# A new prologue and operand layout, and where SyncE issues the loads of second operand halves

## The chip, the core and the metric

The kernel runs on one core of a Trainium2 chip. The metric is device time in microseconds (us); less is better. The core has TensorE (matrix products), VectorE, ScalarE and GpSimd, and SyncE, which issues the DMA transfers; 16 DMA engines carry them.

## What is computed

One transformer layer on x of shape (2, 1024, 128): layer norm, attention of 16 heads of size 8 with a relative position bias and a causal mask, residual; then layer norm, a feed-forward of width 512 (only expert 0 counts), its own residual and layer norm, residual.

```python
q, k, v = (xn @ W.T + b) per head             # 2 batches, 16 heads, 1024 x 8
sim = q @ k.T + rel_emb[bucket(i - j)] * 8 ** -0.5   # no other scale
attn = softmax(where(j > i, -inf, sim)); x = x + (attn @ v) @ Wo.T + bo
t = layernorm(x); h = relu(t @ w1[0] + b1[0]); y = t + h @ w2[0] + b2[0]
out = x + layernorm(y) * gamma + beta
```

## The kernel before

**Operands.** q and k are split into three bfloat16 parts each. All nine products of parts come out of one matmul whose contraction runs over 3 x 3 x 8 = 72 rows of the tiles QA and KA, padded with zeros to 96 rows (KS). Rows 96 and 97 (MROW) of QA hold minus the row maxima, against rows of ones in KA, so that the second pass of scores comes out with the maximum already subtracted. The parts go through a DRAM scratch (qk_scratch): `store_q` and `store_k` write them (L361 to L372), `load_half` (L374) reads one half (512 of 1024 columns) of the operands of one group back, each part at three places. It issues four DMAs: three of 24 rows for QA and one of 72 rows for KA, every row 4 KB.

**Groups.** The 32 pairs of batch and head are worked on as 8 groups of 4 heads. For each group TensorE first makes plain scores in 39 "units" (`unit`, L980): VectorE takes row maxima of them (L759 far from the diagonal, L766 near it, where the bias table NB is added). Unit 13 ("m", 0) and unit 38 ("m", 1) turn the finished maxima of the first and second 512 rows into rows, VectorE copies them to mrow (L754), and `move_m` (L390) sends them to QA. Units that need the second operand half start with unit 10. Then 12 steps of transposed scores follow (L1015), with the bias added by small matmuls from TT (L1032), the exponential on ScalarE (L626) and the product with v (L1044). The units of the next group are interleaved with the steps of this one; the last, unit 38, runs after the group's own first steps. Both `move_m` have to land before the scores of their 512 rows: the second one before step 4.

**SyncE's order.** One queue, in program order. `load` (L440), once per group g: second maxima of g; first maxima of g+1; when step 8 of g has been scored, first half of g+2; when all steps of g have been scored, second half of g+2 and its bias tiles TT from DRAM (L386). From g = 4 on, the gathers of finished heads (L403, L406) stand between these.

**Prologue.** x comes in two DMAs, then a table, the early weights and some rows, and all engines wait for the lot (s_w). Layer norm (L690 to L701), transposes (L932), q/k/v (L938, L944), splits (L712 to L715). The bias table is made as 16 rows of 384, stored to DRAM and loaded back reversed into rev (L414, L422); a flip matmul (L959) and a copy (L598) per two heads give NBH. GpSimd meanwhile sets the pad rows (L482, L485). Group 0's units 0 to 24 (OWN0 = 25) come before its first scores, with the q, k, v of batch 1 (QK_AT) and six of the eight flips (FLIP_AT) between them; `move_m(0, 0, 0)` (L430) is issued behind both loads of group 1 and their TT.

## Time and profile before

| | us |
|---|---|
| median of 3 runs | 405.28 (403.5 to 411.39) |
| the profiled execution | 402.29 |
| its span, first to last instruction | 400.5 |
| mean granted TensorE clock | 0.924 |

The profile is of one execution. Busy time and idle time are given per engine; idle time matters only where that engine is the one the rest waits for. The chain of waits follows the work that ended last back from the end.

### The profile page before, as it was taken

How to read it: one execution, taken by the hardware profiler on the slowest of the kernel's cores; microseconds unless marked ns; L12 is line 12 of the kernel's file. 1: busy time of each engine (PE TensorE's matmuls, PEld its weight loads, DVE VectorE, ACT ScalarE, POOL GpSimd, SP SyncE). 2: the span in 40 equal slices, each digit the busy share in tenths (PEclk: the TensorE clock that was granted, in tenths of full speed). 3: DMA queues.
4: the chain of work that ended last, by engine and by line, in shares of the span. 5: the costliest groups of instructions: out<-in, count | busy, mean ns of one | idle time of the engine just before them, and what ended most of it. 6: DMA issues, size and time to landing. Idle time of an engine off the chain costs nothing.

```text
span 400.5 us, 8158 instructions
## 1 busy us (share of the span) xinstructions
PE 321.0 (80%) x3197; PEld 153.1 (38%) x3197; DVE 287.5 (72%) x960; ACT 184.0 (46%) x258; POOL 69.5 (17%) x78
## 2 busy tenths in 40 slices
PE   0182438396999899799889979988988998999982
PEld 0131215143334335334434433443443344337752
DVE  3985356358668589588678848967875996773986
ACT  1042024131655554575565545556555545873330
POOL 9812035700001000100100100010010000161552
PEclk9996586668699999999999989999998999999998
DMA  8013422410012101201201220331222010100011
GB/s 227 26 53 116 145 90 95 148 64 3 2 43 66 39 18 52 81 1 61 75 12 44 68 64 2 86 88 26 65 79 55 15 16 12 33 2 10 5 52 53
DMA packets 18295, 21.97 MB, mean 55 GB/s; under 512 B 5584, under 2 KB 14960, under 8 KB 18256
## 3 DMA queue, kind: packets, MB, share of 16 engines
q1 hardware_dynamic: 18256, 21.45, 18.5%
q8 instruction: 25, 0.41, 0.4%
q14 instruction: 14, 0.11, 0.1%
HBM read 14.98 MB, written 4.23 MB: 48 GB/s over the span
## 4 chain that ended last, share of the span: by engine, by line
PE 51%; DVE 17%; DMA 15%; ACT 7%; issue 5%; SPq 4%; POOL 1%; DVEq 0%; POOLq 0%; ACTq 0%
PE ps L1015 14%; PE ps L1044 13%; PE ps L1001 13%; DMA QA<-mrow 7%; ACT PT L626 6%; PE ps L1032 5%; DMA qk_scratch<-QS 4%; DVE FM L759 3%; DVE XN L701 2%; DVE junk L766 2%; DMA KA<-qk_scratch 2%; DMA rows<-in_vectors 2%; PE ps L1077 2%; DVE st L836 1%; DVE U L889 1%
## 5 line engine op out<-in xcount | busy, mean ns | idle before, releaser
L626 ACT ACTIVATE PT<-ps 128x1024 f32<-128x1024 f32 (+1 forms) x192 | 145.8, 810 | 132.4 <-PE ps L1032 101.9
L759 DVE TENSOR_REDUCE FM<-ps 128x1 f32<-128x512 f32 (+3 forms) x176 | 108.4, 660 | 29.2 <-PE ps L1001 29.1
L1001 PE MATMUL ps<-KA,QA 96*128 96x256 bf16 (+3 forms) x544 | 108.7, 294 | 17.6 <-DMA KA<-qk_scratch 14.3
L1015 PE MATMUL ps<-QA,KA 98*128 98x512 bf16 (+3 forms) x384 | 99.0, 343 | 25.4 <-DMA QA<-mrow 10.3
L766 DVE CUSTOM_DVE_ANT_0 junk<-ps,NB 128x256 bf16<-128x256 f32 (+1 forms) x224 | 78.8, 403 | 37.3 <-PE ps L1001 37.2
L1044 PE MATMUL ps<-PT,VG 128*16 128x512 f32 (+3 forms) x768 | 86.9, 498 | 0.0
L1001 PEld LDWEIGHTS ps<-KA,QA 96*128 96x128 bf16 x544 | 44.1, 101 | 103.7 <-DVE FM L759 32.9
L1015 PEld LDWEIGHTS ps<-QA,KA 98*128 98x128 bf16 x384 | 32.5, 101 | 52.5 <-ACT PT L626 21.6
L497 POOL COPY NB<-NBH 128x1024 bf16<-128x1024 bf16 x7 | 7.3, 1040 | 212.3 <-PE ps L1044 211.4
L1032 PE MATMUL ps<-TT,flb 128*32 128x176 f16 (+4 forms) x1152 | 38.9, 245 | 0.0
L1032 PEld LDWEIGHTS ps<-TT,flb 128*32 128x32 bf16 x1152 | 21.5, 96 | 17.9 <-issue 17.0
L1044 PEld LDWEIGHTS ps<-PT,VG 128*16 128x16 f32 x768 | 21.5, 97 | 10.3 <-issue 7.2
L766 DVE DVE_READ_ACCUMULATOR2_ANT FM<- 128x1 f32 x256 | 21.3, 83 | 0.0
L766 DVE CUSTOM_DVE_ANT_0 junk<-ps,NBH 128x256 bf16<-128x256 f32 (+1 forms) x32 | 11.2, 403 | 10.5 <-PE ps L1001 10.3
L932 PE MATMUL ps<-early_s,XN 128*128 128x128 f32 x16 | 4.1, 424 | 18.1 <-DVE XN L701 18.1
L1077 PE MATMUL ps<-QS,late_s 128*128 128x512 f32 x32 | 15.8, 611 | 0.8 <-ACT QS L653 0.8
L545 POOL TENSOR_SCALAR tmp<-mv 128x4 f32<-128x4 f32 x8 | 2.3, 285 | 71.3 <-DVE mv L839 71.3
L585 ACT ACTIVATE QS<-ps,early_s 128x512 bf16<-128x512 f32 x8 | 5.5, 687 | 16.4 <-PE ps L938 16.4
L701 DVE TENSOR_SCALAR XN<-X,mv,rs 128x128 f32<-128x128 f32 x16 | 11.9, 1332 | 0.1
L754 DVE COPY mrow<-ps 8x512 bf16<-8x512 bf16 x16 | 6.5, 407 | 7.2 <-PE ps L989 7.2
L938 PE MATMUL ps<-xnT,early_s 128*128 128x512 f32 x16 | 10.5, 769 | 0.0
L932 PEld LDWEIGHTS ps<-early_s,XN 128*128 128x128 f32 x16 | 3.2, 222 | 18.9 <-issue 16.4
(88 smaller groups left out, 255.5 us busy)
## 6 DMA issues: line engine op xcount, KB each, us to landing
QA<-qk_scratch SPq DMA_DIRECT2D x48, 96.0 KB
KA<-qk_scratch SPq DMA_DIRECT2D x16, 288.0 KB
TT<-f_scratch SPq DMA_DIRECT2D x16, 120.0 KB, 7.8
qk_scratch<-QS SPq DMA_DIRECT2D x4, 384.0 KB
qk_scratch<-QS SPq DMA_DIRECT2D x12, 128.0 KB
...
```

Of the source, the lines that this page charges most:

```text
L497: nc.gpsimd.tensor_copy(NB[:, p, :, :], NBH[:, bass.ds(HG * hg, HG), :]).then_inc(s_nb, 1)
L626: nc.scalar.activation(PT[:, s % 3, 2 * q:2 * q + 2, off:off + w], ST[:, q, :, off:off + w], ACT.Exp).then_inc(s_exp, 1)
L701: last = nc.vector.tensor_scalar(XN[:, t, :], X[:, t, :], mv[:, t, 0:1], rs[:, t:t + 1], ALU.subtract, ALU.mult)
L759: nc.vector.tensor_reduce(FM[:, ib, heads[0]:heads[-1] + 1, piece], bank[:, 0:w * len(heads)].rearrange("p (h n) -> p h n", n=w), AX.X, AL ...
L766: last = nc.vector.tensor_tensor_reduce(junk[:, k % NSM, i, 0:w], bank[:, i * w:(i + 1) * w], nb[:, h, 256 - w:256], 1.0, NEG, ALU.add, AL ...
L932: last = nc.tensor.transpose(ps[:, BANK["T", b, half], i * 128:(i + 1) * 128], XN[:, b * TPB + 4 * half + i, :], idf[:, :])
L938: nc.tensor.matmul(ps[:, BANK["QK"[qk], b, c], :], (wq_s, wk_s)[qk][:, :], xnT[:, b, c * IC:(c + 1) * IC], start=True, stop=True).then_inc ...
L1001: last = nc.tensor.matmul(bank[:, i * w + j - j0:i * w + j - j0 + n], QA[0:KS, p, ib // 4, h, (ib % 4) * 128:(ib % 4 + 1) * 128], KA[0:KS, ...
L1015: last = nc.tensor.matmul(ST[:, q, h % 2, off:off + w], KA[0:KST, p, jb // 4, h, (jb % 4) * 128:(jb % 4 + 1) * 128], QA[0:KST, p, ic, h, o ...
L1032: last = nc.tensor.matmul(ST[r0:r0 + 32, q, h % 2, off:off + n], flb[:, 32 * e:32 * e + 32], TT[:, p, h, u0:u0 + n], start=False, stop=Tru ...
L1044: last = nc.tensor.matmul(OV[32 * h:32 * h + 2 * HD, off:off + w], VG[:, p, jb, h, :], PT[:, s % 3, h, off:off + w], start=(jb == 0), stop ...
L1077: last = nc.tensor.matmul(bank, w1_s[:, f * 128:(f + 1) * 128], tT[:, c % 2, :], start=True, stop=True)
```

## The change

The layout drops the zero padding (72 rows, maxima in rows 72 and 73), and its 72 rows are ordered head-size first, so that a half is loaded in six DMAs of 24 rows, each with 8 as its outermost count instead of 3. q and k are stored alike, one DMA each with 128 outermost. The maxima move in one DMA instead of two. The second half of group g+1 is issued in `load(g)`, right behind the second maxima of g. TT is no longer loaded from DRAM for each group: one tile TL holds the table of all heads, and GpSimd copies 4 heads of it. In the prologue x comes in four DMAs; table and early weights are issued from ScalarE's queue; each consumer waits for what it needs; the layer norm runs in pieces of 4 tiles; the bias table is made with 128 partitions and the heads innermost (DRAM runs of 32 bytes when stored, 8 KB when loaded); all flips come before the units; GpSimd sets fewer pads and takes the third part of q. 17 units instead of 25 stand before the first scores. Not shown: buffer and semaphore declarations, the layer norm's renumbering, host code.

```diff
-KS = 96
-MROW = 96
+KS = ROWS
+MROW = ROWS
...
-QK_AT = {3: (0, 0), 5: (0, 1), 8: (1, 0), 10: (1, 1)}
-REMAINDER_AT = {6: (0, 0), 8: (0, 1), 11: (1, 0), 13: (1, 1)}
-FLIP_AT = {14: 2, 15: 3, 16: 4, 18: 5, 19: 6, 20: 7}
+QK_AT = {1: (0, 0), 3: (0, 1), 5: (1, 0), 7: (1, 1)}
+REMAINDER_AT = {4: (0, 0), 6: (0, 1), 8: (1, 0), 10: (1, 1)}
+V_AT = {9: 0, 11: 1}
 RECIP_AFTER = (6, 14, 22, 30)
-OWN0 = 25
+OWN0 = 17
...
+        TL = sb("TL", [128, NEARU, H], FP16)
...
+        R = [PT[:, 1, :, :], OT[:, 4:6, :].rearrange("p g (c n) -> p (g c) n", n=IC)]
+        rev = PT[:, 0, :, :].rearrange("p h n -> p (h n)").bitcast(BF16)
...
-            for b in range(B):
-                sp.dma_start(X[:, b * TPB:(b + 1) * TPB, :], xv[:, b * TPB:(b + 1) * TPB, :]).then_inc(s_x[b], 16)
-                if b == 0:
-                    for dst, src in [(table_s[:, :], table), (early_s[:, :], early),
-                                     (rows[:, :, :], bass.AP(vectors.tensor, 0, [[0, 128], [D, 5], [1, D]]))]:
-                        sp.dma_start(dst, src).then_inc(s_w, 16)
+            for k in range(2 * B):
+                sp.dma_start(X[:, 4 * k:4 * k + 4, :], xv[:, 4 * k:4 * k + 4, :]).then_inc(s_x[k], 16)
+                if k == 1:
+                    sp.dma_start(rows[:, :, :], bass.AP(vectors.tensor, 0, [[0, 128], [D, 5], [1, D]])).then_inc(s_rows, 16)
...
-            def store_q(b, c):
-                sp.wait_ge(s_q3[b], c * 2 + 1)
-                sp.dma_start(bass.AP(qk_d, c * CN + b * GPB * GN, [[IC, 128], [G * GN, NPART], [1, IC]]),
-                             QS[:, b, 0, :, c * IC:(c + 1) * IC]).then_inc(s_qst[b][c], 16)
-            def store_k(b, c):
-                sp.wait_ge(s_q3[b], c * 2 + 2)
-                for a in range(NPART):
-                    sp.dma_start(bass.AP(qk_d, QN + c * CN + (b * GPB * NPART + a) * GN,
-                                         [[NPART * GN, GPB], [IC, HG * HD], [1, IC]]),
-                                 QS[:, b, 1, a, c * IC:(c + 1) * IC]).then_inc(s_qst[b][c], 16)
+            PN = G * GN
+            def store(b, c, qk):
+                sp.wait_ge(s_q3[b][qk], c + 1)
+                sp.dma_start(bass.AP(qk_d, (2 * c + qk) * NPART * PN + b * GPB * GN, [[IC, 128], [PN, NPART], [1, IC]]),
+                             QS[:, b, qk, :, c * IC:(c + 1) * IC]).then_inc(s_qst[b][c], 16)
             def load_half(g, p, c):
-                rows_q = [[0, NPART], [HG * IC, HD], [1, HG * IC]]
-                rows_k = [[0, NPART], [HG * IC, NPART * HD], [1, HG * IC]]
-                for a in range(NPART):
-                    sp.dma_start(QA[24 * a:24 * a + 24, p, c, :, :].rearrange("r h n -> r (h n)"),
-                                 bass.AP(qk_d, g * GN + (c * CN + a * G * GN), rows_q)).then_inc(s_ldqk[p][c], 16)
-                sp.dma_start(KA[0:ROWS, p, c, :, :].rearrange("r h n -> r (h n)"),
-                             bass.AP(qk_d, g * (NPART * GN) + (QN + c * CN), rows_k)).then_inc(s_ldqk[p][c], 16)
-            def load_tt(hg, p):
-                for part in range(2):
-                    sp.dma_start(TT[64 * part:64 * part + 64, p, :, :],
-                                 bass.AP(f16_d, hg * (HG * 2 * BW) + part * BW, [[1, 64], [2 * BW, HG], [1, NEARU]])
-                                 ).then_inc(s_ldt[p], 16)
+                at = g * GN + 2 * c * NPART * PN
+                rows_q = [[HG * IC, HD], [PN, NPART], [1, HG * IC]]
+                rows_k = [[HG * IC, HD], [0, NPART], [1, HG * IC]]
+                for u in range(NPART):
+                    r0 = u * NPART * HD
+                    for tile, start, pattern in ((QA, at, rows_q), (KA, at + (NPART + u) * PN, rows_k)):
+                        sp.dma_start(tile[r0:r0 + NPART * HD, p, c, :, :].rearrange("r h n -> r (h n)"),
+                                     bass.AP(qk_d, start, pattern)).then_inc(s_ldqk[p][c], 16)
             def move_m(p, half, g):
                 wait_apart(sp, s_smf, NU * g + (NU - 1 if half else UNITS.index(("m", 0))) + NSM + 1)
-                for part in range(2):
-                    sp.dma_start(QA[MROW + part:MROW + part + 1, p, half, :, :],
-                                 mrow[4 * part:4 * part + 4, half, :]).then_inc(s_md[half], 16)
+                sp.dma_start(QA[MROW:MROW + 2, p, half, :, :], mrow[:, half, :]).then_inc(s_md[half], 16)
...
-            store_q(0, 0)
             sp.wait_ge(s_f, 1)
-            sp.dma_start(fr_d.ap(), Fr[:, :]).then_inc(s_fst[0], 16)
-            store_k(0, 0)
+            sp.dma_start(bass.AP(fr_d, 0, [[H, 128], [128 * H, XC], [1, H]]), Fr[:, :, :]).then_inc(s_fst[0], 16)
+            sp.wait_ge(s_f, 2)
+            for part in range(2):
+                sp.dma_start(bass.AP(f16_d, part * BW * H, [[H, 128], [128 * H, XC], [1, H]]),
+                             F16[:, part, :, :]).then_inc(s_fst[1], 16)
             sp.wait_ge(s_fst[0], 16)
-            sp.dma_start(rev[:, 0:HG, :], bass.AP(fr_d, 0, [[1, 128], [BW, HG], [1, 256]])).then_inc(s_rev[0], 16)
-            sp.wait_ge(s_f, 2)
-            sp.dma_start(f16_d.ap(), F16[:, :, :]).then_inc(s_fst[1], 16)
-            sp.wait_ge(s_zero, 5)
-            sp.wait_ge(s_qst[0][0], 64)
+            sp.dma_start(rev[:, :], bass.AP(fr_d, 0, [[H, 128], [1, 256 * H]])).then_inc(s_rev, 16)
+            store(0, 0, 0)
+            store(0, 0, 1)
+            sp.wait_ge(s_fst[1], 32)
+            sp.wait_ge(s_zero, 1)
+            sp.wait_ge(s_qst[0][0], 32)
             load_half(0, 0, 0)
-            store_q(0, 1)
-            store_k(0, 1)
-            sp.dma_start(rev[:, HG:H, :], bass.AP(fr_d, HG * BW, [[1, 128], [BW, H - HG], [1, 256]])).then_inc(s_rev[1], 16)
-            sp.wait_ge(s_qst[0][1], 64)
+            for part in range(2):
+                sp.dma_start(TL[64 * part:64 * part + 64, :, :].rearrange("r u h -> r (u h)"),
+                             bass.AP(f16_d, part * BW * H, [[H, 64], [1, NEARU * H]])).then_inc(s_tl, 16)
+            store(0, 1, 0)
+            store(0, 1, 1)
+            sp.wait_ge(s_qst[0][1], 32)
             load_half(0, 0, 1)
-            sp.wait_ge(s_fst[1], 16)
-            load_tt(0, 0)
             load_half(1, 1, 0)
...
-            def load(g, hg, p, sums=()):
+            def load(g, p, sums=()):
                 move_m(p, 1, g)
+                if g:
+                    second_half(g + 1, 1 - p)
                 for k in sums[:1]:
...
                 load_half(g + 2, p, 0)
                 for k in sums[1:]:
                     gather_all(k)
-                wait_apart(sp, s_str, 2 * NSTEP * g + 2 * NSTEP)
-                load_half(g + 2, p, 1)
-                load_tt(hg, p)
+            def second_half(g, p):
+                sp.wait_ge(s_str, 2 * NSTEP * (g - 1))
+                load_half(g, p, 1)
...
             for r in range(0, G // 2 - 2):
                 for p in range(2):
-                    load(2 * r + p, (2 * r + 2) % GPB + p, p)
-            load(G - 4, 2, 0, sums=(0, 1))
-            load(G - 3, 3, 1, sums=(2, 3))
+                    load(2 * r + p, p)
+            load(G - 4, 0, sums=(0, 1))
+            load(G - 3, 1, sums=(2, 3))
             move_m(0, 1, G - 2)
+            second_half(G - 1, 1)
             gather_all(4)
             move_m(1, 0, G - 1)
             gather_all(5)
...
         def _(pool):
-            for pad in (QA, KA):
-                nc.gpsimd.memset(pad[64:96, :, :, :, :].rearrange("p q c h n -> p (q c h n)").bitcast(F32),
-                                 0.0).then_inc(s_zero, 1)
-            pool.wait_ge(s_zero, 2)
-            nc.gpsimd.memset(KA[96:98, :, :, :, :], 1.0).then_inc(s_zero, 1)
-            pool.wait_ge(s_zero, 3)
+            nc.gpsimd.memset(KA[64:KST, :, :, :, :].rearrange("p q c h n -> p (q c h n)"), 1.0).then_inc(s_zero, 1)
+            pool.wait_ge(s_zero, 1)
             nc.gpsimd.memset(VG[:, :, :, :, :], 1.0).then_inc(s_zero, 1)
-            nc.gpsimd.memset(junk[:, :, :, :], 0.0).then_inc(s_zero, 1)
...
+            def copy_tt(hg, p):
+                nc.gpsimd.tensor_copy(TT[:, p, :, :].rearrange("p h u -> p u h"),
+                                      TL[:, :, bass.ds(HG * hg, HG)]).then_inc(s_tt, 1)
...
-            pool.wait_ge(s_w, 16 * NW)
+            for c in range(2):
+                pool.wait_ge(s_mid, 2 * c + 1)
+                q = QS[:, 0, 0, :, c * IC:(c + 1) * IC]
+                nc.gpsimd.tensor_tensor(q[:, 2, :], R[0][:, 2 * c, :], q[:, 1, :], ALU.subtract).then_inc(s_q3[0][0], 1)
...
+            pool.wait_ge(s_tl, 32)
+            copy_tt(0, 0)
+            copy_tt(1, 1)
...
+                    copy_tt((2 * r + 2) % GPB + p, p)
...
+            act.dma_start(table_s[:, :], table).then_inc(s_tab, 16)
+            act.dma_start(early_s[:, :], early).then_inc(s_early, 16)
+            act.wait_ge(s_eps, 1)
+            nc.scalar.activation(warm[:, :], eps[:, :], ACT.Sqrt).then_inc(s_warm, 1)
...
+            def copy_nbh(i):
+                act.wait_ge(s_flip, i + 1)
+                nc.scalar.copy(NBH[:, :, 32 * i:32 * i + 32],
+                               ps[:, FLIP_BANK[i], :].rearrange("p (c h) -> p h c", h=H)).then_inc(s_nbh, 1)
...
             deviation(0)
-            turned(0)
+            turned(0, 0)
             deviation(1)
-            first_parts(0)
+            act.wait_ge(s_early, 16)
+            first_parts(0, 0)
+            turned(0, 1)
+            first_parts(0, 1)
             copy_v(0)
-            copy_nbh(0, 2)
-            turned(1)
-            first_parts(1)
+            for i in range(4):
+                copy_nbh(i)
+            deviation(2)
+            deviation(3)
+            for i in range(4, 8):
+                copy_nbh(i)
+            turned(1, 0)
+            turned(1, 1)
+            first_parts(1, 0)
+            first_parts(1, 1)
             copy_v(1)
-            copy_nbh(2, 8)
             act.wait_ge(s_warm, 1)
-            nc.scalar.activation(warm[:, :], cols[:, 3:4], ACT.Exp).then_inc(s_warm, 1)
...
-            act.wait_ge(s_q3[1], 4)
...
+                mid = nc.vector.tensor_copy(q[:, 1, :], R_).then_inc(s_mid, 1)
+                if qk:
+                    dve.wait_ge(s_mid, k + 1)
+                    nc.vector.tensor_tensor(q[:, 2, :], R_, q[:, 1, :], ALU.subtract).then_inc(s_q3[0][1], 1)
+            def bias_table():
+                got = ps[:, BANK["F", 0, 0], 0:2 * XC * H].rearrange("p (a c h) -> p a c h", a=2, c=XC)
+                mask = [mk_s[:, a, :, :].broadcast_to([128, XC, H]) for a in range(2)]
+                dve.wait_ge(s_tp, TASK["F", 0, 0] + 1)
+                nc.vector.scalar_tensor_tensor(Fr[:, :, :], got[:, 1, :, :], SCALE, mask[1],
+                                               ALU.mult, ALU.add).then_inc(s_f, 1)
+                own(nc.vector.scalar_tensor_tensor(Ff[:, :, :], got[:, 0, :, :], SCALE / BSC, mask[0],
+                                                   ALU.mult, ALU.add))
+                own(nc.vector.tensor_copy(F16[:, 0, :, :], Ff[:, :, :]))
+                own(nc.vector.tensor_tensor(Ff[:, :, :], Ff[:, :, :], F16[:, 0, :, :], ALU.subtract))
+                nc.vector.tensor_scalar(F16[:, 1, :, :], Ff[:, :, :], LSC, None, ALU.mult).then_inc(s_f, 1)
...
+            dve.wait_ge(s_early, 16)
+            bias_table()
             stats0(1)
-            dve.wait_ge(s_w, 16 * NW)
+            norm(1)
...
-            split(0, 0, 0)
...
-            dve.wait_ge(s_zero, 5)
+            for c in range(2):
+                for qk in range(2):
+                    split(c, qk)
+            for k in range(2, 4):
+                stats0(k)
+            for k in range(2, 4):
+                norm(k)
...
+            def task_f():
+                for k in range(2 * XC):
+                    last = nc.tensor.matmul(ps[:, BANK["F", 0, 0], k * H:(k + 1) * H],
+                                            oh_s[:, k // XC, (k % XC) * 128:(k % XC + 1) * 128], emb_s[:, :],
+                                            start=True, stop=True)
+                last.then_inc(s_tp, 1)
...
-                pe.wait_ge(s_rev[i >= 2], 16)
                 if i >= 2:
                     pe.wait_ge(s_nbh, i - 1)
-                if FLIP_BANK[i] == 2:
-                    pe.wait_ge(s_r, 4)
-                nc.tensor.matmul(ps[:, FLIP_BANK[i], :], flb[:, 64:192], rev[:, 2 * i:2 * i + 2, :],
+                nc.tensor.matmul(ps[:, FLIP_BANK[i], :], flb[:, 64:192], rev[:, 512 * i:512 * i + 512],
...
-            pe.wait_ge(s_w, 16 * NW)
+            pe.wait_ge(s_tab, 16)
+            task_f()
+            pe.wait_ge(s_early, 16)
             task_t(0, 0)
+            task_qks(0, 0)
             task_t(0, 1)
-            task_qks(0, 0)
-            task_f(0)
-            task_f(1)
             task_qks(0, 1)
             task_v(0, 0)
             task_v(0, 1)
             pe.wait_ge(s_f, 2)
             pe.wait_ge(s_ov, 2)
             pe.wait_ge(s_cst, 2)
-            task_flip(0)
-            task_flip(1)
-            pe.wait_ge(s_q3[0], 2)
+            pe.wait_ge(s_rev, 16)
+            for i in range(8):
+                task_flip(i)
+            pe.wait_ge(s_q3[0][1], 1)
...
-                    pe.wait_ge(s_md[ic], 32 * g + 32)
...
-                            pe.wait_ge(s_ldt[1 - p], 32 * load)
+                            pe.wait_ge(s_tt, g + 2)
...
-            pe.wait_ge(s_q3[0], 4)
-            pe.wait_ge(s_nbh, 2)
+            pe.wait_ge(s_q3[0][1], 2)
+            pe.wait_ge(s_nbh, 8)
...
+                if k in V_AT:
+                    if k == min(V_AT):
                         pe.wait_ge(s_r, 2)
-                    task_v(1, k - 12)
-                if k in FLIP_AT:
-                    task_flip(FLIP_AT[k])
+                    task_v(1, V_AT[k])
                 if k in HALF_UNITS:
-                    pe.wait_ge(s_ldqk[0][HALF_UNITS[k]], 64)
...
-            pe.wait_ge(s_ldt[0], 32)
+            pe.wait_ge(s_tt, 1)
```

## Rows read from the trace of the kernel before

**Rows 1.** Page, part 1: busy time, share of the span, instructions, for TensorE and VectorE.

```profile
PE 321.0 (80%) x3197; PEld 153.1 (38%) x3197; DVE 287.5 (72%) x960; ACT 184.0 (46%) x258; POOL 69.5 (17%) x78
```

**Rows 2.** Chain that ended last, 0 to 140 us: start us, length us, what.

```profile
28.30 5.78 DMA qk_scratch<-QS
...
39.56 10.39 DMA qk_scratch<-QS
...
52.24 8.56 DMA KA<-qk_scratch
...
72.50 6.10 issue
...
95.99 2.57 DMA QA<-mrow
...
131.65 4.49 DMA QA<-mrow
```

**Rows 3.** Timeline, 0 to 28 us: start us, busy us, engine, line, operation, xcount.

```profile
7.73 6.92 POOL L485 MEMSET KA<- 2x8192 bf16 x1
...
9.31 9.77 DVE L701 TENSOR_SCALAR XN<-X,mv,rs 128x128 f32<-128x128 f32 x8
...
15.98 1.09 PE L932 MATMUL ps<-early_s,XN 128*128 128x128 f32 x4 [15.98 <-DVE XN L701]
```

**Rows 4.** Line view of L701: duration ns min/median/max.

```profile
L701 DVE TENSOR_SCALAR XN<-X,mv,rs x16: 329/346/5422, 9.3 to 35.7; 128x128 f32<-128x128 f32 x16
```

**Rows 5.** DMA view, whole run: KB each, median us from issue to landing.

```profile
early_s<-in_early SPq DMA_DIRECT2D x1, 356.0 KB, 5.4
...
fr_scratch<-Fr SPq DMA_DIRECT2D x1, 12.0 KB, 2.3
```

**Rows 6.** Windows of 1 us: busy by engine, clock, DMA share of 16 engines, GB/s.

```profile
47.00:48.00 1.00, 1.00 (x2) 0.15 (x1) 1.00 (x7) 0.00 (x0) 0.00 (x0) 0.50 1.04 319
...
55.00:56.00 1.00, 0.00 (x0) 0.00 (x0) 0.90 (x5) 0.00 (x0) 0.81 (x1) 1.00 0.77 197
...
57.00:58.00 1.00, 0.00 (x0) 0.00 (x0) 0.00 (x0) 0.00 (x0) 0.00 (x0) 0.50 0.19 78
...
256.00:257.00 1.00, 1.00 (x14) 0.55 (x15) 1.00 (x2) 0.03 (x1) 0.00 (x0) 1.00 0.43 102
```

**Rows 7.** Timeline, 34 to 79 us: SyncE issues, and TensorE where it starts again.

```profile
34.16 2.26 SPq L379 DMA_DIRECT2D QA<-qk_scratch  x3
...
45.08 1.44 PE L1001 MATMUL ps<-KA,QA 96*128 96x128 bf16 x8 [7.43 <-DMA KA<-qk_scratch]
...
66.88 2.91 SPq L394 DMA_DIRECT2D QA<-mrow  x2
...
78.60 1.01 PE L1015 MATMUL ps<-QA,KA 98*128 98x512 bf16 x2 [6.10 <-issue]
```

**Rows 8.** Windows: the stretch after the first scores, and two of the later groups.

```profile
78.60:95.34 16.74, 14.22 (x137) 6.62 (x138) 9.71 (x30) 5.19 (x8) 0.00 (x0) 0.74 0.18 64
...
169.45:202.79 33.34, 30.84 (x364) 13.71 (x365) 25.95 (x94) 19.00 (x26) 1.38 (x2) 1.00 0.14 45
...
236.98:271.77 34.79, 32.23 (x364) 14.27 (x365) 26.00 (x94) 19.20 (x26) 1.38 (x2) 0.95 0.22 56
```

**Rows 9.** Waits, whole run: us in total, times, longest us.

```profile
PE ps L1015 <- DMA QA<-mrow: 10.3, 7, 2.3
```

**Rows 10.** Timeline, 126 to 142 us: SyncE's issues, TensorE's last wait and unit matmuls.

```profile
126.26 0.69 SPq L381 DMA_DIRECT2D KA<-qk_scratch  x1
...
130.93 1.35 SPq L394 DMA_DIRECT2D QA<-mrow  x2
...
136.18 0.61 PE L1015 MATMUL ps<-QA,KA 98*128 98x512 bf16 x2 [1.63 <-DMA QA<-mrow]
...
141.88 0.33 PE L1001 MATMUL ps<-KA,QA 96*128 96x384 bf16 x1
```

**Rows 11.** Groups by line and form, GpSimd: busy us, mean ns of one, idle before.

```profile
L497 POOL COPY NB<-NBH 128x1024 bf16<-128x1024 bf16 x7 | 7.3, 1040 | 212.3 <-PE ps L1044 211.4 <-ACT NBH L598 0.9
```

171 lines of the change are left out of this document (72 added, 99 removed).

## The prediction

> **What bounds the kernel now.** I read the page's busy shares first, then the chain that ended last, then the waits of TensorE, and last the DMA shares in short windows. TensorE is busy for 80% of the span and VectorE for 72% [rows 1]; nothing in the change takes matmul columns or row maxima away, so a gain can only come from idle time of TensorE. The reader should find it in two places. The first is the start: TensorE's first scores begin at 78.60 us [rows 7], and the chain up to there runs mostly over DMAs: stores until 34.1 and 49.9, a KA load until 60.8, and 6.1 us of waiting from 72.5 [rows 2]. The second is small and comes in each group: seven waits for the maxima's way through DMA (QA<-mrow), 10.3 us together [rows 9]. The groups themselves have little air: 30.84 us of TensorE in 33.34 us [rows 8].
>
> **Why the loads are slow.** While only operand loads run, 0.19 of the DMA engines are busy, at 78 GB/s [rows 6]: that is 3 of 16, 26 GB/s each. The patterns of `load_half` have an outermost count of 3 in DRAM. Where 128 stands outermost (the rev load) the share is 1.04 and the rate 319 GB/s, and gathers of 8 rows reach 0.43, or 7 engines [rows 6]. A half is 6 x 96 KB = 590 thousand bytes, so at 78 GB/s it takes 7.5 us, and the KA share that ended at 60.8 fits (8.56 us from its issue, with QA's in front) [rows 2]. With 8 outermost I expect 8 engines: 12 KB on each per DMA, 12.3/26 = 0.47 us, less than SyncE's issue of 2.26/3 = 0.75 us [rows 7]. So a half becomes limited by its issues: 6 x 0.72 = 4.3 us (0.69 for a KA issue [rows 10], 0.75 for QA), and about 2 us to land.
>
> The Trainium skill gives a rule for this (DMA: Bandwidth & Descriptors, Why a DMA increments its semaphore by 16 and not by 1): the number of engines is the largest up to 16 that divides the outermost counts of both sides. By it the old loads get 3, with which the share of 0.19 agrees, the new ones 8, and k's stores 16 instead of 4. The sum by it is the same.
>
> **The prologue, step by step.** (a) The first x pieces are half as large. early_s landed 5.4 us after its issue [rows 5]; issued at about 1.3 us from ScalarE's queue it is there near 7. Statistics of 4 tiles, root and reciprocal end near 7 as well. The first normalisations took 9.77 us for 8 tiles, one of them 5422 ns against a median of 346 [rows 3, 4]: it began at 9.31, while GpSimd's KA memset ran from 7.73 to 14.65, and came free with it. After the change one such memset (6.9 us, the same 8192 columns) starts at 0.7 and ends at 7.7, then comes VG. Four tiles are done near 9.3, and the first transposes move from 15.98 [rows 3] to 9.3: 6.7 us. (b) The bias table is five VectorE instructions of 48 columns where there were five of 384, near 1.2 us; its stores issue at 9.8 to 11.4 and land by 13 to 15 (2.3 us for fr before [rows 5]), behind the rest of the 2.4 MB of inputs. rev, 1 MB at about 300 GB/s (319 in [rows 6]), lands near 19.5, and eight flips and copies at 0.7 us each, with two roots, end near 26.5. (c) Split of the first halves ends near 17.1, GpSimd doing q's third part beside it. Two stores of 384 KB over all engines: landed at 22 instead of 34.1 [rows 2]. (d) Half 0: 22 + 4.3 + 2.3 = 28.8, against 45.08 [rows 7]. The flips' path ends at about the same time. (e) TL (0.98 MB) and the stores of the second halves (0.79 MB) issue by 28.3, and 1.77 MB take 6 us: landed near 34.5 instead of 49.9. Half 1 of group 0: 34.5 + 4.3 + 2.3 = 41. The ten units that need only half 0, with four projections of batch 1 between, lasted from 45.08 until VectorE fell idle after 56 [rows 6, 7], 11 us, so they end near 40, just in time. (f) Both halves of group 1 keep SyncE until 34.5 + 3 x 4.4 = 47.7, and the first maxima stand behind them: 47.7 + 0.7 + 2.6 [rows 2] = 51. Before, they were issued from 66.88 to 69.8 and landed at 78.6, behind three slow halves [rows 7]. So the first scores start at **51, 27.6 us earlier**.
>
> Of this something is given back. Units 17 to 24, eight of them, 6 of 0.69 us and 2 of 0.85 on VectorE, now stand behind the first scores. The stretch up to the second maxima had 16.74 us with 9.71 of VectorE and 14.22 of TensorE [rows 8]; 8 units add 5.8 and about 3.1. TensorE would have 17.3 us, and with waits at each engine's change I take 19.2: **+2.5** (0 if they all fall into idle time, 5.8 if none does).
>
> **The groups.** The second maxima of a group were issued at 130.93 and landed at 136.18, 4.49 us after the issue, because the QA and KA pieces of the second half, issued up to 126.95, were still in the same three engines [rows 2, 10]. With nothing in front it was 2.57 [rows 2], and one DMA instead of two saves 0.6 us of issue. So they land near 134.1, before TensorE runs out of work at 134.55 (136.18 less 1.63 [rows 10]). The six waits after the first are 1.3 to 2.3 us each; I take all 10.3 us [rows 9] as gone, and 1.7 of clock: group 236.98 to 271.77, which began behind a wait of 2.3, shows a mean clock of 0.95 and 32.23 us of TensorE against 30.84 [rows 8], and one more group is like it. As TensorE and VectorE then meet more often, 1.5 comes back: **-10.5**.
>
> What is late next is the second half itself. It is now issued at 131.6 in that group, behind the maxima, instead of ahead of them; 6 x 0.72 and 2.3 put it at 138.2. The first unit that needs it started at 141.88 [rows 10], which becomes 140.2: 2 us of slack. I cost it at nothing; with three engines it would land at 141.5 and cost 1.3 us in each of six groups. Behind it on SyncE stand the first maxima of the next group (due at the group's end) and, from g = 4, eight gathers: first maxima were issued 9 us after the gathers' end, so 4.3 us more are hidden. The first half of g+2 waits for step 8 as before. The wait that fell away on TT is now one on GpSimd: a copy of 960 columns in 2-byte steps. The nearest row is NB, 1024 columns in 1.04 us [rows 11], and GpSimd is otherwise idle for 32 us a group; at ten times that price it is still hidden. KS of 72 instead of 96 saves nothing, since a matmul's time goes by its columns. The end behind the last scores is untouched.
>
> **A price with two ends.** The table's stores now go in runs of 32 bytes, 1152 of them, 72 per engine. At 480 bytes (TT) 197 GB/s at a share of 0.77 are 410 runs in 12.3 engine-us, 30 ns each [rows 6]. So 2.2 us at that price, and nothing above the 2.3 us of the old fr store at the other end; I take 2.2 beside the x loads, and 4.4 for the range. It would delay rev and the flips, which have about 1 us of slack against half 0.
>
> The Trainium skill (DMA: Bandwidth & Descriptors, Specifications) says that below 512 bytes an engine reads, modifies and writes. That speaks against this change; no row shows a 32-byte run, and twice the price of a run would put the sum some 2 us higher.
>
> **Sum.** 402.3 (the profiled execution) - 27.6 + 2.5 - 10.5 = 366.7, so **367 us**. The median of the runs shown is 0.7% above the profiled execution; I leave that in the range.
>
> **Rivals.** *Loads no faster (three engines, or ports shared in the tile).* Speaks for it: QA and KA pieces still go to only 24 partitions, and gathers of 8 rows move only 102 GB/s at 7 engines [rows 6]. Then half 0 lands at 22 + 2 + 7.5 = 31.5, half 1 at 34.5 + 9.5 = 44, both of group 1 by 59, and first scores at 60 instead of 51; with 1.3 us in six groups: 367 + 9 + 8 = 384. *The table path sets the first unit.* If 32-byte stores and rev come 8 us later than I say, flips end at 34.5 and everything behind half 0 slips by 6, but half 1 and the group-1 loads do not wait for it: units then are late against the maxima, 373. *The gain in the groups is not there,* because another engine holds the first step back once the maxima are early: VectorE has 25.95 us in 33.34 [rows 8], which speaks against it. 367 + 10.5 = 377. *More than I say:* the clock stays up in group 0 (0.74 of full in 78.60 to 95.34 [rows 8]) and less of the 8 units shows: 355. *Slower than before:* the new pattern puts a DMA on one engine. Then a half takes 590/26 = 22.7 us, and each group's second half lands at 131.6 + 25, 16 us late in six groups. With a half of h us the start costs 3 x (h - 4.3) more and the groups 6 x (h - 6.3), so it decides from h = 9.6 us, that is at two engines or fewer; with one engine it is 367 + 55 + 98 = 520 us. Against it speaks that gathers with 8 outermost show 7. *It does nothing:* would need the prologue to hang on something the change leaves alone; the chain there shows none.
>
> **Chances.** Forecast 0.60 (360 to 375), table path 0.10, no gain in the groups 0.08, slow loads 0.09, more 0.09, slower 0.02, nothing 0.02. The likeliest is 367. Leaving out the tails gives 354 to 382. What a measurement of this kernel can tell from no change is about 2%, 8 us; so faster 0.95, same 0.03, slower 0.02.
>
> **What the profile after would show.** First transposes at 9 to 10 us; first unit at 27 to 32; first scores at 48 to 55; a DMA share of 0.3 to 0.5 where only halves are loaded, not 0.19; QA<-mrow at 2 to 2.7 us in the chain or gone from TensorE's waits; groups of 31.8 to 32.3 us; no wait of the first w=384 unit for KA. A first unit behind the flips, or one that waits for KA in each group, makes the forecast wrong by the sums above.

## The result, and the profile after

The changed kernel takes 391.88 us (median, 388.27 to 401.49), the one before 405.58 beside it: ratio 0.964 [0.958, 0.971]. That is faster, but by 14 us where the forecast had 35.6 (402.3 to 366.7). Two runs of the changed kernel, 400.29 and 401.49 us, had a lower granted clock than the others and are not in the ratio. The profiled execution has a span of 386.5 us against 400.5. I read it against the one before at the same five marks: the first scores, and the issue of the second maxima of the first, second and last group. The first of each pair is the kernel before.

| stretch | before | after | difference | forecast |
|---|---|---|---|---|
| start to first scores | 78.60 | 49.53 | -29.1 | -27.6 |
| to second maxima of group 0 | 16.74 | 23.23 | +6.5 | +2.5 |
| to those of group 1 | 35.59 | 38.64 | +3.1 | |
| to those of group 7 (6 groups) | 205.12 | 210.69 | +5.6 | -10.5, with the row above |
| to the end | 64.45 | 64.41 | 0 | 0 |

So the prologue did what it was to do, and 23 us are missing behind it (15.2 lost where 8.0 were to be won). What TensorE waits for has changed. Its longest waits behind the start, in the changed kernel (line, releaser, us in total, times, longest):

```profile
PE ps L1004 <- DVE MC L796: 18.4, 7, 2.7
PE ps L1030 <- ACT PT L635: 7.7, 18, 0.7
PE ps L1016 <- DMA KA<-qk_scratch: 4.0, 1, 4.0
PE ps L1030 <- issue: 4.0, 1, 4.0
```

The waits for QA<-mrow of [rows 9] are gone, as forecast. In their place stand seven waits for MC (before there was one, of 1.7 us), the small tile in which VectorE splits the finished maxima in two before TensorE turns them into rows (L1004). The groups of costly instructions on the page have two lines that stand out (busy us, mean ns of one):

```profile
L489 POOL COPY TT<-TL 128x960 f16<-128x960 f16 x8 | 35.9, 4543 | 8.4 <-DMA TL<-f_scratch 8.4
...
L794 DVE CAST MC<-NM 128x16 bf16<-128x16 f32 x16 | 23.9, 1495 | 0.6
```

A cast of 16 columns has a mean of 1495 ns; VectorE's own view of that line says 174/175/3376 ns (minimum, median, maximum), so some are done in 0.175 us and others take twenty times that. Six of the sixteen take 3.3 to 3.4 us, one for each copy of the table at a group's end; a seventh, in the prologue, takes 2.3. The end of group 1's units in the timeline (start us, busy us, engine) shows one of the six:

```profile
104.46 1.04 POOL L486 COPY NB<-NBH 128x1024 bf16<-128x1024 bf16 x1 [46.38 <-PE ps L1059]
105.43 4.51 POOL L489 COPY TT<-TL 128x960 f16<-128x960 f16 x1
106.57 0.20 DVE L791 TENSOR_REDUCE NM<-FM 128x16 f32<-128x48 f32 x1
106.81 3.38 DVE L794 CAST MC<-NM 128x16 bf16<-128x16 f32 x1
109.53 0.63 POOL L481 COPY VG<-VA 128x256 f32<-128x256 f32 x1
110.22 0.18 DVE L796 TENSOR_TENSOR MC<-NM,MC 128x16 bf16<-128x16 f32 x1
110.54 0.38 PE L1004 MATMUL ps<-idb,MC 128*8 128x128 bf16 x4 [2.74 <-DVE MC L796]
...
111.40 0.67 SPq L383 DMA_DIRECT2D QA<-mrow  x1
```

The reader is to see three things. GpSimd's copy of the bias table is not 1 us but 4.51. While it runs, VectorE's reduction is quick (0.20 us), but the cast behind it ends only at 110.19, 0.25 us after that copy and together with GpSimd's next one. And TensorE stands still for 2.74 us before L1004.

The stall costs more than itself. These are the group from 180.24, the one from 214.66, and the first 15 us of the latter (columns: us, PE, PEld, DVE, ACT, POOL busy, granted clock, DMA share, GB/s):

```profile
180.24:214.66 34.42, 30.78 (x369) 13.74 (x368) 28.90 (x94) 19.00 (x26) 5.71 (x3) 1.00 0.11 36
214.66:255.19 40.53, 36.93 (x368) 15.82 (x367) 29.39 (x94) 19.32 (x26) 5.73 (x3) 0.83 0.18 44
...
214.66:219.66 5.00, 5.00 (x65) 2.69 (x65) 2.31 (x16) 1.75 (x4) 0.00 (x0) 0.58 0.26 78
219.66:224.66 5.00, 5.00 (x24) 2.02 (x23) 2.41 (x10) 3.11 (x4) 0.00 (x0) 0.50 0.39 86
224.66:229.66 5.00, 5.00 (x21) 1.53 (x19) 2.30 (x7) 2.11 (x3) 0.00 (x0) 0.55 0.09 13
```

The same work takes 6.1 us longer in one of the groups: TensorE is busy 36.93 us instead of 30.78, since it is at 1.2 GHz instead of 2.4 for 13.7 of 15 us, right behind one of the stalls.

**The theory** to be tested: all that is missing in the groups comes from this copy, because some of VectorE's small instructions can't run beside it (cast 3.38 us, reduction 0.20). The Trainium skill (SBUF — State Buffer, Who interferes with whom) has a rule that fits each of the lines: GpSimd and VectorE share one pair of ports as an exclusive lock; VectorE's copies and casts in their two-port modes are shut out, and so is an instruction of VectorE with two SBUF inputs against a GpSimd instruction that reads SBUF; a reduction never is. **The rivals:** the cast waits for something else that ends at the same time; the new place of the second halves in SyncE's queue delays something; and the loads themselves are not what was gained.

### The profile page after: what moved, and what is told of

It reads as the page before. It is cut to its first block, busy times and chain, and to the rows that moved or that the text cites. A ratio compares the mean times of both kernels' runs of the same rounds, so it can differ in the third digit from the quotient of the medians.

```text
span 386.5 us, 8175 instructions
## 1 busy us (share of the span) xinstructions
PE 328.4 (85%) x3205; PEld 156.8 (41%) x3205; DVE 299.3 (77%) x961; ACT 184.1 (48%) x260; POOL 96.4 (25%) x85
## 4 chain that ended last, share of the span: by engine, by line
PE 58%; DVE 23%; ACT 6%; DMA 5%; issue 4%; SPq 2%; POOL 1%; DVEq 0%; POOLq 0%
PE ps L1016 16%; PE ps L1030 15%; PE ps L1059 14%; ACT PT L635 6%; PE ps L1047 6%; DVE MC L794 5%; DVE junk L780 4%; DVE FM L773 3%; DMA qk_scratch<-QS 3%; SPq L377 2%; PE ps L1092 2%; PE ps L1004 1%; DVE st L850 1%; DVE U L903 1%; DMA X<-in_x 1%
## 5 line engine op out<-in xcount | busy, mean ns | idle before, releaser
L1016 PE MATMUL ps<-KA,QA 72*128 72x256 bf16 (+3 forms) x544 | 111.6, 302 | 5.7 <-DMA KA<-qk_scratch 4.0
L1030 PE MATMUL ps<-QA,KA 74*128 74x512 bf16 (+3 forms) x384 | 99.3, 347 | 12.4 <-ACT PT L635 7.7
L1059 PE MATMUL ps<-PT,VG 128*16 128x512 f32 (+3 forms) x768 | 89.3, 511 | 0.0
L1016 PEld LDWEIGHTS ps<-KA,QA 72*128 72x128 bf16 x544 | 45.7, 103 | 94.2 <-DVE FM L773 30.1
L1030 PEld LDWEIGHTS ps<-QA,KA 74*128 74x128 bf16 x384 | 33.8, 102 | 37.5 <-ACT PT L635 19.6
L1047 PE MATMUL ps<-TT,flb 128*32 128x176 f16 (+4 forms) x1152 | 39.5, 248 | 0.0
L489 POOL COPY TT<-TL 128x960 f16<-128x960 f16 x8 | 35.9, 4543 | 8.4 <-DMA TL<-f_scratch 8.4
L794 DVE CAST MC<-NM 128x16 bf16<-128x16 f32 x16 | 23.9, 1495 | 0.6
L1004 PE MATMUL ps<-idb,MC 128*8 128x128 bf16 x64 | 6.5, 228 | 18.5 <-DVE MC L796 18.4
L1004 PEld LDWEIGHTS ps<-idb,MC 128*8 128x8 bf16 x64 | 3.7, 87 | 28.4 <-issue 22.6
L859 DVE TENSOR_TENSOR QS<-ps,X 128x512 f32<-128x512 f32 x4 | 2.7, 683 | 10.5 <-PE ps L1083 10.5
```

Of the source, the lines that this page charges most:

```text
L489: nc.gpsimd.tensor_copy(TT[:, p, :, :].rearrange("p h u -> p u h"), TL[:, :, bass.ds(HG * hg, HG)]).then_inc(s_tt, 1)
L794: nc.vector.tensor_copy(m0, nm3).then_inc(s_dm, 1)
L1004: last = nc.tensor.transpose(bank.bitcast(BF16)[0:8, i * 128:(i + 1) * 128], MC[:, half, i, :, :].rearrange("p q h -> p (q h)"), idb[:, :])
L1016: last = nc.tensor.matmul(bank[:, i * w + j - j0:i * w + j - j0 + n], QA[0:KS, p, ib // 4, h, (ib % 4) * 128:(ib % 4 + 1) * 128], KA[0:KS, ...
L1030: last = nc.tensor.matmul(ST[:, q, h % 2, off:off + w], KA[0:KST, p, jb // 4, h, (jb % 4) * 128:(jb % 4 + 1) * 128], QA[0:KST, p, ic, h, o ...
L1047: last = nc.tensor.matmul(ST[r0:r0 + 32, q, h % 2, off:off + n], flb[:, 32 * e:32 * e + 32], TT[:, p, h, u0:u0 + n], start=False, stop=Tru ...
```

## Experiments on the copy

**The copy moved.** The changed kernel; each group's copy of the table waits until VectorE has split the second maxima.

```diff
                     copy_nb((2 * r + 2) % GPB + p, p)
+                    pool.wait_ge(s_ms, 2 * g + 4)
                     copy_tt((2 * r + 2) % GPB + p, p)
```

> The changed kernel, with one wait added: GpSimd makes the TT copy of a group's end only after VectorE has subtracted the second maxima (L796), so that the 4.5 us copy no longer runs beside the cast of the maxima (L794). Theory A (the copy holds something that VectorE's SBUF-to-SBUF cast needs, and the cast waits until it ends): every cast is 0.17 us, the seven TensorE waits for the maxima's transposes (18.4 us together) fall to under 5, the groups go from 34.4 to about 32, and the time from 391.9 to 371 to 377 us. Rival B (the groups are longer because SyncE's new order or the six DMAs disturb them, and the cast is long for that reason): casts stay at 3.3 us and the time within 3 us of 391.9.

Measured: 366.82 us (363.67 to 367.62), ratio 0.905 [0.899, 0.912] to the kernel before. In its timeline the copy is as long as ever and the cast is short:

```profile
108.34 0.18 DVE L795 CAST MC<-NM 128x16 bf16<-128x16 f32 x1
108.55 0.18 DVE L797 TENSOR_TENSOR MC<-NM,MC 128x16 bf16<-128x16 f32 x1
108.79 4.55 POOL L489 COPY TT<-TL 128x960 f16<-128x960 f16 x1 [1.77 <-DVE MC L797]
```

One line gives 25 us, 4 more than the best that I had written, and of the seven waits for MC one is left:

```profile
PE ps L1005 <- DVE MC L797: 2.2, 1, 2.2
```

Between the second maxima of group 1 and those of group 7 it takes 191.5 us where the changed kernel takes 210.7: five groups are 2.7 us shorter each, which is the stall, and one of these another 6.1, which is the clock (the last group is 0.3 longer). A group is now 31.75 us; the forecast had 31.8 to 32.3.

**A reduction in place of the cast.** The changed kernel, copy where it is; the upper part of the split is made by a reduction from FM that writes bfloat16.

```diff
-                    nc.vector.tensor_copy(m0, nm3).then_inc(s_dm, 1)
+                    nc.vector.tensor_reduce(m0, FM[:, 4 * half:4 * half + 4, :, :], AX.X, ALU.max,
+                                        negate=True).then_inc(s_dm, 1)
```

> The changed kernel, with the copy where it is, but the bfloat16 maxima m0 come from a tensor_reduce over FM (one SBUF input, bfloat16 output) instead of a cast from NM. Theory A1 (only the two-port copy mode of VectorE is shut out): the reduce takes 0.2 us beside the copy, and so does the subtraction after it, which has two SBUF inputs; time 371 to 378 us. Theory A2 (an instruction with two SBUF inputs is shut out by a GpSimd instruction that reads SBUF as well): the stall of about 3.2 us moves to the subtraction, and the time stays within 3 us of 391.9. Rival B: as A2 in time, with the long instruction still the one that makes m0.

Measured: 382.50 us (382.13 to 383.69), ratio 0.947 [0.942, 0.952]. The timeline of the same place:

```profile
105.82 4.51 POOL L489 COPY TT<-TL 128x960 f16<-128x960 f16 x1
106.96 0.20 DVE L791 TENSOR_REDUCE NM<-FM 128x16 f32<-128x48 f32 x1
107.20 0.20 DVE L794 TENSOR_REDUCE MC<-FM 128x16 bf16<-128x48 f32 x1
107.44 2.28 DVE L797 TENSOR_TENSOR MC<-NM,MC 128x16 bf16<-128x16 f32 x1
109.83 0.23 PEld L1005 LDWEIGHTS ps<-idb,MC 128*8 128x8 bf16 x4 [2.57 <-issue]
109.86 0.38 PE L1005 MATMUL ps<-idb,MC 128*8 128x128 bf16 x4 [1.68 <-DVE MC L797]
109.90 0.65 POOL L481 COPY VG<-VA 128x256 f32<-128x256 f32 x1
```

Both reductions pass beside the copy, and the stall moves to the subtraction, whose two inputs lie in SBUF. So it is not the time or the place that blocks but the kind of instruction, which speaks against a rival that names another cause. The subtraction ends at 109.72, just before VG's copy starts and 0.6 us before the record of the table's copy ends (records of GpSimd are rough); the cast came free only with VG's copy, 0.66 us after that had begun. TensorE's waits for MC fall from 18.4 to 12.0 us. Theory A2 had the place right and not the time: with each stall 1 us shorter the kernel is 9 us under 391.9, not within 3.

**The copy added to the kernel before.** An extra GpSimd copy of 960 columns of NBH with the same steps, per group and at the same place; its output is used by nothing.

```diff
+            def extra(p, n):
+                ...
+                src = NBH[:, :, :].rearrange("p h c -> p (h c)")[:, 0:NEARU * H].rearrange("p (u h) -> p u h", h=H)
+                nc.gpsimd.tensor_copy(spare[:, :, :].rearrange("p h u -> p u h"), src[:, :, 4 * p:4 * p + 4]).then_inc(s_ex, 1)
...
                     copy_nb((2 * r + 2) % GPB + p, p)
+                    extra(p, g)
```

> The kernel before, with one more GpSimd instruction per group (six in all): a copy of 960 two-byte columns in 32-byte steps behind the NB copy, into a tile that nothing reads. Theory A: the copy takes 4.5 us, the cast of the second maxima takes about 3.3 us in six groups, the maxima land 3 us later, and the kernel before becomes 3 us longer in each of six groups: 405.6 + 16 to 20 = 422 to 426 us. Rival B: within 3 us of 405.6.

Measured: 412.60 us (410.89 to 414.48), ratio 1.021 [1.015, 1.027]. The direction is right and the size is less than half of what I wrote. The copy is 4.53 us and the cast 3.40 here too, and TensorE waits for MC as long as in the changed kernel:

```profile
PE ps L998 <- DVE MC L791: 18.0, 7, 2.8
```

but the 10.3 us of waiting for QA<-mrow [rows 9] are no longer on its list. The maxima of the kernel before were held up by the second half in front of them anyway, and the two waits lie over each other: the spans differ by 8.6 us, about what 18.0 less 10.3 leaves. A stall is worth its length only where nothing else waits at the same place.

**No copy.** The changed kernel without GpSimd's copies of the table: TensorE's bias matmuls read the table TL where it lies, in steps of 32 bytes.

```diff
-                    copy_tt((2 * r + 2) % GPB + p, p)
...
-                                                        TT[:, p, h, u0:u0 + n], start=False, stop=True,
+                                                        TL[:, u0:u0 + n, HG * (g % GPB) + h], start=False, stop=True,
...
```

> The kernel of e1 without GpSimd's TT copies: TensorE reads the bias straight from TL, in steps of 32 bytes. If TensorE reads 2-byte columns in 32-byte steps at its usual rate: L1047's matmuls stay at 0.24 us, casts at 0.17 us, and the time at 364 to 367 us. If the steps cost it: the bias matmuls (39 us in all) grow to twice that or more, and the time goes to 390 us or above.

Measured: 429.81 us (428.14 to 431.17), ratio 1.068 [1.058, 1.078]. The cast is short (174/174/293 ns), but the copy was there for a reason. The bias matmuls on the page of the changed kernel, then of this one:

```profile
L1047 PE MATMUL ps<-TT,flb 128*32 128x176 f16 (+4 forms) x1152 | 39.5, 248 | 0.0
```

```profile
L1043 PE MATMUL ps<-TL,flb 128*32 128x176 f16 (+4 forms) x1152 | 117.0, 493 | 0.0
```

Their median duration goes from 239 to 497 ns, and busy time from 39.5 to 117.0 us.

**The copy walked the other way.** The changed kernel, copy at its old place, same 960 columns, heads outermost: written one after the other, read in steps of 32 bytes.

```diff
-                nc.gpsimd.tensor_copy(TT[:, p, :, :].rearrange("p h u -> p u h"),
-                                      TL[:, :, bass.ds(HG * hg, HG)]).then_inc(s_tt, 1)
+                nc.gpsimd.tensor_copy(TT[:, p, :, :],
+                                      TL[:, :, bass.ds(HG * hg, HG)].rearrange("p u h -> p h u")).then_inc(s_tt, 1)
```

> The changed kernel with the table copy in the same place, of the same 960 columns, but walked with the heads outermost: written one after the other and read in steps of 32 bytes, where the changed kernel writes in steps and reads runs of 4 heads. Theory A (the steps make the copy dear, on whichever side they lie): 3.5 us or more, the cast beside it as long, 388 us or more. Rival B (GpSimd is slow at scattered writes alone): about 1 to 2 us for the copy, and a time near 370 us, since the cast is then held for no more than that.

Measured: 365.47 us (363.85 to 367.21), ratio 0.906 [0.896, 0.915]. The rival was right. GpSimd's view of the copy, and VectorE's of the cast:

```profile
L489 POOL COPY TT<-TL x8: 1914/1934/1948, 32.8 to 261.9; 128x960 f16<-128x960 f16 x8
...
L794 DVE CAST MC<-NM x16: 174/176/590, 37.9 to 296.1; 128x16 bf16<-128x16 f32 x16
```

1.93 us instead of 4.51 for the same elements. The walk changes two things at once, though: which side has the long steps, and how many elements lie innermost (240 instead of 4). That the written steps are what is dear is the likelier reading; no run takes the two apart. The copy ends before the cast has waited half a microsecond, and that is as good as moving it.

## Experiments on the loads and on SyncE's order

**Three outermost.** The changed kernel with its six DMAs of 24 rows, but 3 outermost in each and 8 inside.

```diff
-                rows_q = [[HG * IC, HD], [PN, NPART], [1, HG * IC]]
-                rows_k = [[HG * IC, HD], [0, NPART], [1, HG * IC]]
+                rows_q = [[0, NPART], [HG * IC, HD], [1, HG * IC]]
+                rows_k = [[PN, NPART], [HG * IC, HD], [1, HG * IC]]
...
-                    for tile, start, pattern in ((QA, at, rows_q), (KA, at + (NPART + u) * PN, rows_k)):
+                    for tile, start, pattern in ((QA, at + u * PN, rows_q), (KA, at + NPART * PN, rows_k)):
```

> The changed kernel, where each of the six DMAs of a half carries 3 as its outermost count (the parts) and 8 inside, instead of 8 and 3. Same bytes, same number of DMAs, all products as before, in another order of rows. If the outermost count sets the number of engines: DMA share 0.19 in stretches with halves only (0.3 to 0.5 in the changed kernel), a half takes 7.5 us; the first unit moves from 27.7 to about 30.5 us, the first scores from 49.5 to about 58, and the time from 391.9 to 400 or a little more. If the number of engines does not hang on it: within 2 us of 391.9.

Measured: 429.25 us (424.16 to 432.61), ratio 1.058 [1.049, 1.067], 37 us above the changed kernel and beyond what I wrote. Two stretches of it, one microsecond in which only a half is loaded and one group, show how:

```profile
155.00:156.00 1.00, 1.00 (x26) 0.64 (x26) 1.00 (x4) 0.22 (x1) 0.00 (x0) 1.00 0.19 78
...
127.45:167.95 40.50, 36.94 (x366) 15.79 (x365) 29.36 (x94) 19.32 (x26) 5.70 (x3) 0.83 0.08 31
```

The share of 0.19 and the 78 GB/s of [rows 6] are back; in the changed kernel the share is 0.41 at 148 GB/s in 43 to 44 us, in the middle of a half, and the issues set the pace. The first scores start at 65.08, not 49.53, after waits for KA of up to 5.8 us. From the second maxima of group 0 to those of group 7 it takes 28 us more (277.2 against 249.3), but little of that is waiting for a late half. Only two groups have a wait for KA, of 2.4 and 2.2 us; with 3.4 us at 1.2 GHz in each they cost 4 us apiece, where I had priced a late half at 1.3. The group shown has none. It starts behind the stall that the copy makes, and then looks like the long group of the changed kernel (40.53 us, 0.83):

```profile
126.59 0.38 PE L1004 MATMUL ps<-idb,MC 128*8 128x128 bf16 x4 [2.75 <-DVE MC L796]
```

Four of the six stalls are followed by 13.7 us at 1.2 GHz here, one in the changed kernel, and at 6.1 us each the three more are 18 of the 28. Whether the slow loads bring them no run tells; the version with the old place of the second half, below, has three with quick loads.

**Only the loads.** The kernel before, its loads alone cut into six DMAs with 8 outermost.

```diff
-                rows_q = [[0, NPART], [HG * IC, HD], [1, HG * IC]]
-                rows_k = [[0, NPART], [HG * IC, NPART * HD], [1, HG * IC]]
+                rows_q = [[HG * IC, HD], [0, NPART], [1, HG * IC]]
+                rows_k = [[HG * IC, HD], [GN, NPART], [1, HG * IC]]
...
```

> The kernel before with one thing of the change alone: its operand loads in six DMAs of 24 rows with 8 outermost instead of four DMAs with 3. Prologue, padding, the load of TT, SyncE's order are the old ones, and there is no copy of the table. Theory A (the loads' engines are the whole of the steady part and a share of the prologue): four halves ahead of the first maxima become some 3 us shorter each, of which the layer norm's and the stores' time keeps the rest, first scores near 66 to 70 us instead of 78.6, the seven waits for QA<-mrow (10.3 us) fall to under 3, and the time is 384 to 390 us. Rival B (the loads' engine count matters only together with the rest): 398 us or more.

Measured: 376.10 us (374.89 to 377.42), ratio 0.931 [0.923, 0.938]: better than both theories, and 16 us faster than the whole change. First scores start at 67.34, 11.3 us earlier; the waits for QA<-mrow are gone; a group takes 31.75 us:

```profile
117.20:148.95 31.75, 30.67 (x365) 13.71 (x366) 25.76 (x94) 19.00 (x26) 1.38 (x2) 1.00 0.16 48
```

So seven tenths of what the change can give is in these lines (27.4 of 38.5 us of span, the latter with heads outermost), and what I had counted too low is again the clock. From the second maxima of group 0 to those of group 7 this kernel needs 223.99 us and the one before 240.71: 10.3 for the waits, and 6.4 more, most of it from three of the groups, in which TensorE was busy 1.5 to 2 us longer in the kernel before at a mean clock of 0.86 to 0.95.

**The second half at its old place**, in two versions: in the kernel with the moved copy, and in the changed kernel as it is.

```diff
-                if g:
-                    second_half(g + 1, 1 - p)
...
+                wait_apart(sp, s_str, 2 * NSTEP * g + 2 * NSTEP)
+                load_half(g + 2, p, 1)
...
-            second_half(G - 1, 1)
```

> The kernel of e1 with the second operand half of group g+2 issued at its old place, behind the last scores of group g and so ahead of the second maxima of g+1. If SyncE's new order is what lets the maxima land early: QA<-mrow takes over 3 us again and TensorE waits for it in six groups by 0.5 to 1.5 us each, 370 to 375 us. If the eight engines alone do it (six DMAs now take 4.3 us to issue from the group's end, and are through before the maxima are ready): within 1.5 us of e1's 366.8.

> The changed kernel with its table copy where it is, and only SyncE's order put back: the second half of group g+2 behind the last scores of group g, as before the change. With the copy moved out of the way this order was worth nothing that shows (365.4 against 366.8 us). Theory A (the copy is all that goes wrong in the groups, and the loads with 8 engines are quick in either place): 390 to 393 us, groups of 34.4 us. Rival B (the new order helps while the cast is late, or the maxima now queue behind the second half): 395 us or more, and QA<-mrow comes back among TensorE's waits.

Measured: 365.40 us (364.24 to 367.18), ratio 0.908 [0.899, 0.917], against 0.905 [0.899, 0.912] with the new place; and 393.94 us (387.87 to 400.79), 0.960 [0.948, 0.971], against 0.964 [0.958, 0.971]. The second median lies between my two ranges, so it decides nothing; the ratio does. The new order of SyncE's queue moves nothing that can be measured, and neither trace has a wait of TensorE for QA<-mrow: with eight engines a half is out of the way of the maxima from either place. That rival falls too. The trace of the second version is of its run of 400.79 us. Three of its six stalls are followed by 13.7 us at 1.2 GHz; three of its groups take 40.5, 40.5 and 38.5 us, the others between them 34.4 to 34.5.

**The first scores.** In the kernel with the moved copy: 25 units ahead of them instead of 17 (OWN0); the first maxima issued between the two halves of group 1 instead of behind both; and both together.

```diff
-OWN0 = 17
+OWN0 = 25
...
             load_half(1, 1, 0)
-            load_half(1, 1, 1)
             move_m(0, 0, 0)
+            load_half(1, 1, 1)
```

> The kernel of e1 (366.8 us) with 25 instead of 17 units ahead of group 0's first scores, as the kernel before had. Open is why the stretch from the first scores to the second maxima's issue grew from 16.7 to 23.2 us in the changed kernel. Theory C (the eight units are the reason: TensorE and VectorE sat idle ahead of the first scores anyway, 4.5 us in e1): first scores move from 50.5 to 52 to 53 us, the stretch shrinks by 4 to 5, and the time falls by 1 to 3 us. Theory D (the stretch is long because TensorE runs at the lower clock for 15 us there): the stretch shrinks by less than the first scores move, and the time stays within 1 us or rises.

> The kernel of e1 with the first maxima of group 0 issued between the two halves of group 1 instead of behind both. In e1 they are ready at about 45 us and wait for SyncE until 47. If the queue holds the first scores: they move from 50.5 to about 49 us, and the time by 0 to 2 us. If group 1's second half is then late: a wait of TensorE for KA shows in group 0.

> The copy moved behind the second maxima, 25 units ahead of the first scores, and the first maxima issued between the halves of group 1's loads. Singly the last two gave 362.3 and 364.5 us against 366.8. Theory A (the two take the same stretch, the wait before the first scores, so they do not add): 361 to 363 us. Rival B (they add): 358 to 360 us. With 25 units ahead the maxima are issued before TensorE comes to the first scores either way, which speaks for A.

Measured: 362.34 us (360.81 to 367.18), ratio 0.900 [0.891, 0.910]; 364.51 (363.61 to 365.19), 0.906 [0.898, 0.913]; and both 361.02 (359.71 to 364.08), 0.894 [0.886, 0.903]. With the first maxima ahead, the first scores start at 47.07 us instead of 50.50, but the next eight units still stand behind them. With both, they start at 49.88, but the second maxima of group 0 are issued at 67.06 instead of 70.29. Whether the two steps add is not shown: 361.02 lies in the range for "they do not", but the medians fall by 4.5 and 2.3 us singly and by 5.8 together, and the intervals are wider than the difference. The last is the fastest kernel of the study, 11% below the one before; its interval overlaps that of the moved copy (0.905 [0.899, 0.912]).

## Why the forecast was wrong, by its own steps

**Right: the prologue.** First transposes at 8.96 us (9.3 forecast), first unit at 27.72 (28.8), first maxima issued at 46.65 (47.7), first scores at 49.53 (51). The first four normalisations take 2.45 us beside GpSimd's 6.92 us memset, where eight took 9.77 [rows 3]. The flips' last copy ends at 26.84 (26.5). What set the first unit is neither path alone: TensorE waits 2.63 us for ScalarE's copies of the flips, then goes from the last flips (25.12) through the second batch's transposes (26.01) to the unit without a wait, so half 0 was there in time. The price with two ends, the stores in runs of 32 bytes, fell nearer the low end: fr landed 2.9 us after its issue (issued at 8.96, its readback at 11.89), where 2.2 and 4.4 were the ends and the old store took 2.3. The Trainium skill's rule on transfers under 512 bytes (DMA: Bandwidth & Descriptors, Specifications) shows here in no more than these 0.6 us of one store.

**Right: the engines of a load, and the wait for the maxima.** Eight outermost, halves limited by their issues of 0.65 to 0.83 us, no wait for QA<-mrow. The steady group of 31.75 us, at the low end of my 31.8 to 32.3, appears in every version whose copy is moved. Where the copy does little harm, as with heads outermost, the sum can be laid beside the forecast, stretch by stretch:

| | forecast | heads outermost |
|---|---|---|
| to the first scores | -27.6 | -29.2 |
| to second maxima of group 0 | +2.5 | +4.6 |
| groups | -10.5 | -13.8 |
| to the end | 0 | -0.1 |
| sum | -35.6 | -38.5 |

**Wrong: "The nearest row is NB, 1024 columns in 1.04 us [rows 11], and GpSimd is otherwise idle for 32 us a group; at ten times that price it is still hidden."** Two mistakes stand in this sentence. The price: 4.51 us, since NB's copy [rows 11] runs along both tiles, and this one takes four elements at a time and writes in steps of 480 bytes, not 2. That alone would be harmless. The second is the one that decides: I asked whether GpSimd had the time, and not whether VectorE could work meanwhile. The copy's place, behind NB's, is just where VectorE has three small instructions between the last maximum of a group and TensorE's next step. In medians it cost 25 us (391.9 against 366.8). In the two profiled executions it is 20.7: 13.4 in five stalls of 2.7, 6.1 in one stretch at the lower clock, and 1.5 ahead of the second maxima of group 1, less 0.3 in the last group. The other 4 us of the medians no trace shows. The profiled execution of the changed kernel was its quickest; those near the median record a mean clock of 0.908 to 0.912 where it has 0.920, so more time at 1.2 GHz is the likely reason.

The evidence was among my rows: a normalisation of 5422 ns beside a median of 346 [rows 4], free when GpSimd's memset ended [rows 3]. I used it to explain the prologue and took it for a matter of the prologue. A stall of that kind comes wherever the two meet, and the change added eight meetings.

**Wrong: that no rival said it.** "The gain in the groups is not there, because another engine holds the first step back once the maxima are early" had the right place and 0.08 of the chance, but its reason against (VectorE busy for 25.95 of 33.34 us) looks at the sum and not at the one instruction that comes last.

**Off in size: the eight units behind the first scores.** +2.5 was 19.2 us for a stretch that took 23.23 (21.38 with heads outermost). TensorE has 17.58 us of work in the latter, where I had 17.3, so there it is the waits that I made too small: 3.8 us, where I had 1.9. In the changed kernel TensorE is busy 19.76 us, and the 2.2 more are the clock: the stretch follows a wait of 4.0 us and opens at the lower level.

```profile
50.00:55.00 5.00, 4.28 (x26) 1.53 (x25) 1.38 (x2) 1.94 (x2) 5.00 (x11) 0.50 0.63 213
55.00:60.00 5.00, 5.00 (x33) 1.88 (x31) 3.30 (x11) 1.51 (x2) 3.08 (x8) 0.50 0.00 0
60.00:65.00 5.00, 5.00 (x41) 2.75 (x39) 4.03 (x12) 0.80 (x2) 0.00 (x0) 0.50 0.01 3
```

That is 15 us at 1.2 GHz, where before the first 5 us were at 0.50 and the next already at 0.63 on average. Why the clock came back later here, and within 10 us with heads outermost, no run of mine tells.

**What stays open.** The kernel with only the loads changed comes to its first scores 18 us later than the one with heads outermost, and the other gives 7 of them back up to group 1 (17.33 against 21.38 us, then 32.53 against 35.63). I know it as a lower clock (0.90 against 0.83 in the second stretch) and eight more units behind the first scores, and can't divide it further. Nor was a kernel tried that has heads outermost together with 25 units ahead. The parts of the new prologue other than the loads were never run singly, so what each gives of the 29 us is read from the trace and not shown. And why the lower clock comes behind some stalls and not behind others is open.
